# Last mixture of a four-part network: four places instead of two between TensorE and ScalarE, with TensorE three halves ahead

## The chip, the cores and the metric

The kernel runs on one core of one Trainium2 chip. The metric is the device time of one execution in microseconds, as the median of several runs. A core has five engines with instruction streams of their own that meet only through semaphores: TensorE (PE: matmuls and transposes, results to PSUM), VectorE (DVE), ScalarE (ACT), GpSimd (POOL, here mostly issuing indirect DMAs) and SyncE (SP, issuing plain DMAs). PSUM has eight banks of 128 partitions x 512 fp32.

## The reference

Two layers of cross attention and a feed-forward mixture over x of 2 x 1024 tokens of 256 values; what matters here is the last part, a mixture with three routers:

```python
x_flat = x.reshape(B * T, D)
x_addr = x_flat @ P_w.T
dw1 = _route_dense(x_addr @ U1.T, K, TAU)   # top 3 of 12, softmax over the 3
dw2 = _route_dense(x_addr @ U2.T, K, TAU)
dw3 = _route_dense(x_addr @ U3.T, K, TAU)
h = _apply_mixture(x_flat, dw1, W1)         # sum_e dw[n,e] * (W[e] @ x[n])
h = jax.nn.gelu(h, approximate=False)
y = _apply_mixture(h, dw2, W2)
y = y + dw3 @ b2
```

with W1 of 12 x 1024 x 256, W2 of 12 x 256 x 1024, all in fp32. Each of 2048 tokens goes to three experts of the 12, by one router for W1 and by another for W2.

## The kernel before, in words

The mixture (`top3_mixture`) sorts the 2048 x 3 pairs of token and expert by expert into LT = 59 tiles of 128 rows, so that a tile has one expert (`owner`). The hidden vector of 1024 values is worked on in two halves of HH = 512.

**First products** (`expand(n)`, L2046; n from 0 to 117, the first 59 with the first half of W1, then 59 with the second half, "the second part"). GpSimd gathers token rows, TensorE transposes them (L2034, first part only) and multiplies a tile with its expert's weights into a bank of `psH` (n % 2). ScalarE copies the bank (`products`, L2141) into one of four places `po` in `shared`, and SyncE stores it to DRAM (L2299). TensorE waits for the copy of the product before last (`po_ready`, n - 1). Meanwhile GpSimd gathers three rows per token from what is stored (L1692, `W<-p_d,f_rows`), VectorE adds them up with their weights (`combine`, L2246 to L2249), and SyncE stores the sums (L2311). There are 16 sums per half; those of the first half run beside the first products' second part, those of the second half beside the first 52 halves of the second products.

Between the two come 16 small matmuls for `dw3 @ b2` (`bias`, L2063) through the banks of `psT` and `psY`.

**Second products.** The 59 tiles are worked on as 118 half tiles ("halves") in an order that `turns_of_products` makes: first the first half of tiles 0 to 51 (turns "first", 52 halves), then the second halves of these ("second"), and among them, spread evenly, seven whole tiles (52 to 58, "whole", two halves each). For each half m:

- GpSimd fetches the hidden rows from DRAM (`hidden(n)`, L1692 `shared<-h_d` or `sel<-h_d`) into one of up to seven seats `hg` (five in the later part). A fetch waits until the seat's last half has been transposed (`hT_mm`, `u.free`).
- TensorE transposes it (`turn_hidden(m)`, L2072, four transposes into `psV[m % 2]`), after waiting for the fetch (`hg_ld`) and for the gelu of m - 2 (`hT_ready`).
- ScalarE applies the gelu out of PSUM into `hT[m % 2]` (`hidden_T`, L2146), after waiting for the contraction of m - 2 (`y_mm`).
- TensorE contracts it with W2 (`contract(m)`, L2089, four matmuls of 128x256, eight records in the trace) into `psY[n % 2]`, n the turn.
- For the turns "first", ScalarE copies the result into `y_part` (`first_part`, L2150). For "second", VectorE adds it (L2268), for "whole" it copies (L2265); then GpSimd scatters the tile's rows to DRAM (`scatter`, L1988).

The orders are written out by hand. On TensorE:

```python
turn_hidden(0)
for m in range(TILES):          # 118
    if m + 1 < TILES:
        turn_hidden(m + 1)
    contract(m)
```

ScalarE has the same order with `hidden_T(m + 1)` ahead of `first_part(m)`. GpSimd alternates one hidden fetch with one gather for the sums in the first parts (`three`), and from turn 58 on `hidden(n)` with `scatter(n - 6)`; after the last fetch the last six scatters follow. After all scatters the pairs come back from DRAM and are weighted and added (L2125, L2276, L2281), and the tiles are stored.

PSUM is full: `psT`, `psH`, `psV` and `psY` of two banks each. During the first products `psV` holds the routing's counts and lists, and SBUF has little room left.

Of the kernel before, what the change touches and what calls it, by code (L numbers as in the profile page):

```python
# [6 lines left out]
ALU = mybir.AluOpType  # L7
# [53 lines left out]
LATE = 4  # L61
TT = B * NT
# [66 lines left out]
def build(nc, t, out):  # L129
# [41 lines left out]
    with ctx:  # L171
# [9 lines left out]
        def attention_weights(stack, a):  # L181


            w = sb(stack, a + "W", [P, 4, KD, D])
            return [w] + [w[:, i] for i in range(4)] + [sb(stack, a + n, shape) for n, shape in (
                ("bk", [P, KD]), ("bq", [P, KD]), ("bvr", [1, D]))]
# [44 lines left out]
        def bias_row(eng, l, done):  # L231
            eng.dma_start(att[l][7][:, :], t[f"a{l}_bv"].rearrange("(a d) -> a d", a=1)).then_inc(done, 16)
# [115 lines left out]
        def value_products(pe, Wv, bvr, place):  # L348
            for b in range(B):
                for k in range(KD):  # L350
                    pe.matmul(place(b), ctxT[:, k, b * S2:(b + 1) * S2], Wv[:, k, :], start=k == 0, stop=False)
                mm = pe.matmul(place(b), ones[0:1, 0:S2], bvr[:, :], start=False, stop=True)
# [1163 lines left out]
        def top3_mixture(W, W1, W2, Pw, U, w_ld, w1_ld, w2_ld, load_w1_part, finite):  # L1516
# [9 lines left out]
            with st:  # L1526
# [21 lines left out]
                under = sb(st, "f_under", [P, E1 + 1, E1])  # L1548
                spread = sb(st, "f_spread", [P, E1 + 1, E1])
# [5 lines left out]
                first = sb(st, "f_first", [P, TT])  # L1555
# [10 lines left out]
                pdiv = sb(st, "f_pdiv", [P, TOP, TT])  # L1566
                pmod = sb(st, "f_pmod", [P, TOP, TT])
# [167 lines left out]
                with main:  # L1735
# [11 lines left out]
                    hT = xh.rearrange("p (s k n) -> p s k n", s=2, k=KQ)  # L1747
# [4 lines left out]
                    b2 = sb(main, "f_b2", [P, D])  # L1752
# [202 lines left out]
                    with nc.Block() as block:  # L1955
# [68 lines left out]
                        def _(pe):  # L2024
# [13 lines left out]
                            def expand(n):  # L2038
# [5 lines left out]
                                wait(pe, po_ready, n - 1)  # L2044
                                for k in range(KD):
                                    mm = pe.matmul(psH[:, n % 2, :], xTk[:, i, k, :], W1[c][:, e, k, :],  # L2046
# [19 lines left out]
                            def turn_hidden(m):  # L2066
# [3 lines left out]
                                wait(pe, hT_ready, m - 1)  # L2070
                                for k in range(KQ):
                                    mm = pe.transpose(psV[:, m % 2, k * P:(k + 1) * P],  # L2072
# [3 lines left out]
                            def contract(m):  # L2076
# [6 lines left out]
                                if n < 2:  # L2083
                                    pe.wait_ge(b_done, TT)
                                elif m == u.half:
                                    pe.wait_ge(ya_ready, min(n - 1, FIRST))
                                    wait(pe, yo_ready, n - 1 - FIRST)
                                for k in range(KQ):
                                    mm = pe.matmul(psY[:, n % 2, 0:D], hT[:, m % 2, k, :], W2[c][:, e, k, :],  # L2089
# [361 lines left out]
```

## Time and profile before

| | us |
|---|---|
| three timed runs, median (lowest, highest) | 1159.28 (1157.64, 1161.54) |
| span of the profiled execution | 1216.9 |
| first products' second part (734 to 840) | 106 |
| second products (849.0 to 1187.3) | 338.3 |
| of these: first parts, to 1009 | 160 |
| of these: second parts and whole tiles | 178 |
| return of the pairs, end (from 1188) | 29 |

The profile is one execution, recorded instruction by instruction. TensorE is its busiest engine (90% of the span). A record's span does not include the time at which its semaphore is seen elsewhere; that shows in when the next engine starts. Idle time of an engine is put down to what ended it.

### The profile page before, as it was taken

What the parts mean: (1) busy time and instruction counts of PE and PEld (TensorE: products, weight loads), DVE (VectorE), ACT (ScalarE), POOL (GpSimd) and SP (SyncE); (2) the same over time, 40 slices, a digit from 0 to 9 for tenths busy, and PEclk for the clock granted to TensorE, in tenths of its full rate; (3) what the DMA queues carried; (4) which work ended last, traced back from release to release, by engine and by line L of the source; (5) the groups of instructions that cost most, each with busy time, mean ns of one, the idle gap of its engine ahead of it and who ended that gap; (6) DMA issues with size and microseconds to landing.
All of it is one profiled execution on the core that took longest, in us unless ns stands there. A gap on an engine that the chain in (4) does not pass through costs nothing.

```text
span 1216.9 us, 19171 instructions
## 1 busy us (share of the span) xinstructions
PE 1094.3 (90%) x6013; PEld 817.2 (67%) x6013; DVE 552.3 (45%) x1120; ACT 420.3 (35%) x833; POOL 381.8 (31%) x421
## 2 busy tenths in 40 slices
PE   7999899998999999999399999998677888888885
PEld 4888744888998878887244443444566777776773
DVE  4988766764444446776872501333122211111114
ACT  1566544321112225664244432332222232222220
POOL 0221100000220011011154434552666646665650
PEclk8999999998999999999599999998898899999998
DMA  7000130004980029001155578997778865444437
GB/s 208 2 0 0 33 139 1 1 1 161 345 286 9 0 66 382 27 0 47 37 180 200 186 211 295 349 364 276 249 253 278 269 201 179 134 131 142 132 121 281
DMA packets 93410, 187.89 MB, mean 154 GB/s; under 512 B 14109, under 2 KB 34575, under 8 KB 93340
## 3 DMA queue, kind: packets, MB, share of 16 engines
q1 hardware_dynamic: 65346, 109.45, 25.4%
q0 software_dynamic: 23696, 73.69, 19.6%
q10 hardware_dynamic: 4298, 3.81, 1.0%
q8 instruction: 45, 0.74, 0.2%
q14 instruction: 25, 0.20, 0.0%
HBM read 133.56 MB, written 55.44 MB: 155 GB/s over the span
## 4 chain that ended last, share of the span: by engine, by line
PE 40%; issue 4%; DMA 4%; DVE 2%; another core or an unknown queue 2%; ACT 1%; SPq 0%; POOL 0%; POOLq 0%; DVEq 0%; ACTq 0%
PE f_psY L2089 18%; PE f_psH L2046 15%; PE f_psV L2072 4%; DMA W<-in_f_W1T 2%; DMA W<-p_d 2%; PE f_psT L2034 1%; ACT a_W L2146 1%; DVE W L1650 1%; PE f_psV L83 1%; DMA shared<-h_d,f_half_toks 0%; PE f_psH L1929 0%; PE f_psV L1662 0%; SPq L2343 0%; DVE f_xTk L2268 0%
## 5 line engine op out<-in xcount | busy, mean ns | idle before, releaser
L2089 PE MATMUL f_psY<-W,a_W 128*128 x944 | 240.7, 401 | 57.4 <-issue 35.6
L2089 PEld LDWEIGHTS f_psY<-W,a_W 128*128 128x128 f32 x944 | 179.4, 200 | 87.0 <-issue 65.4
L2046 PE MATMUL f_psH<-W,f_xTk 128*128 x472 | 215.5, 596 | 5.7 <-ACT shared L2141 2.0
L2046 PEld LDWEIGHTS f_psH<-W,f_xTk 128*128 128x128 f32 x472 | 84.1, 190 | 96.0 <-issue 95.6
L2146 ACT ACTIVATE a_W<-f_psV 128x512 f32<-128x512 f32 x118 | 70.0, 598 | 155.8 <-PE f_psV L2072 94.8
L2141 ACT ACTIVATE shared<-f_psH 128x512 f32<-128x512 f32 x118 | 70.4, 597 | 142.1 <-PE f_psH L2046 109.5
L1692 POOL DMA_INDIRECT W<-p_d,f_rows x96 | 95.0, 989 | 64.7 <-issue 24.7
L1692 POOL DMA_INDIRECT shared<-h_d,f_half_toks x90 | 87.6, 974 | 85.4 <-DMA p_d<-shared 25.6
L2246 DVE TENSOR_SCALAR a_W<-W,f_wt 128x512 f32<-128x512 f32 x32 | 15.9, 496 | 204.7 <-DMA W<-p_d,f_rows 147.6
L2268 DVE TENSOR_TENSOR f_xTk<-f_psY,f_xTk 128x256 f32<-128x256 f32 x52 | 21.7, 424 | 144.1 <-PE f_psY L2089 112.5
L1692 POOL DMA_INDIRECT a_W<-xn_d,f_toks x59 | 57.6, 975 | 88.9 <-PE f_psT L2034 54.3
L1510 POOL DMA_DIRECT2D m_eos<-m_eo x32 | 16.8, 527 | 202.0 <-DVE m_eo L1407 200.7
L700 POOL TENSOR_TENSOR X<-X,a_bob 128x256 f32 x32 | 24.4, 765 | 162.7 <-DVE a_xn L579 82.6
L1988 POOL DMA_INDIRECT p_d<-f_xTk,f_dest x59 | 58.4, 990 | 45.9 <-DVE f_xTk L2268 25.5
L2072 PE MATMUL f_psV<-ident,shared 128*128 128x128 f32 x360 | 56.5, 282 | 2.3 <-DMA shared<-h_d,f_half_toks 1.7
L1360 PE MATMUL m_psE<-m_eos,m_wu 128*128 128x256 f32 x256 | 57.8, 380 | 0.4 <-DVE m_wu L1436 0.4
L1131 PE MATMUL m_psL<-m_seT,shared 128*128 128x512 f32 x128 | 57.4, 592 | 0.0
L310 POOL TENSOR_TENSOR rstd<-veps,mhalf 128x8 f32<-128x8 f32 (+4 forms) x8 | 13.6, 1696 | 136.7 <-DVE veps L303 136.7
L2072 PEld LDWEIGHTS f_psV<-ident,shared 128*128 128x128 f32 x360 | 46.9, 147 | 13.1 <-DMA shared<-h_d,f_half_toks 2.6
L735 ACT ACTIVATE a_pT<-a_psP 128x256 f32<-128x256 f32 (+2 forms) x96 | 46.8, 490 | 20.2 <-PE a_psP L838 19.0
L2150 ACT ACTIVATE f_xTk<-f_psY 128x256 f32<-128x256 f32 x52 | 20.0, 384 | 93.5 <-PE f_psY L2089 54.0
L1360 PEld LDWEIGHTS m_psE<-m_eos,m_wu 128*128 128x128 f32 x256 | 47.5, 190 | 6.5 <-DVE m_wu L1436 0.7
(299 smaller groups left out, 1867.8 us busy)
## 6 DMA issues: line engine op xcount, KB each, us to landing
p_d<-shared SPq DMA_DIRECT2D x118, 256.0 KB
W<-in_f_W1T SPq DMA_DIRECT2D x24, 512.0 KB, 8.8
W<-in_f_W2T SPq DMA_DIRECT2D x24, 512.0 KB
m_wg<-in_m_Wg SPq DMA_DIRECT2D x16, 512.0 KB, 4.0
m_wu<-in_m_Wu SPq DMA_DIRECT2D x16, 512.0 KB, 5.2
m_wd<-in_m_Wd SPq DMA_DIRECT2D x16, 512.0 KB, 6.1
h_d<-a_W SPq DMA_DIRECT2D x32, 256.0 KB
W<-p_d SPq DMA_DIRECT2D x16, 384.0 KB, 9.2
```

What stands on the lines that cost most here:

```text
L700: pool.tensor_tensor(X[:, s, j], X[:, s, j], bob[:, :], ALU.add).then_inc(xb_ready, 1)
L735: act.activation(pT[:, s, full[0]:full[-1] + 1, :].rearrange("p c n -> p (c n)"), psP[:, g % 2 if g < 2 else 1, 0:len(full) * P], ACT.Copy ...
L1131: mm = pe.matmul(psL[:, n % 2, q * BANK:(q + 1) * BANK], xT[:, n % 2, k, :], seT[:, k, q * BANK:(q + 1) * BANK], start=k == 0, stop=k == K ...
L1360: mm = pe.matmul(psY[:, s, 0:D], ecT[:, s, c, :], eos[:, s, c, :], start=c == 0, stop=c == CS - 1)
L1692: pool.indirect_dma_start(place, None, source, bass.IndirectOffsetOnAxis(ap=index, axis=0)).then_inc(done, 16)
L1988: pool.indirect_dma_start(p2_rows, bass.IndirectOffsetOnAxis(ap=dest[:, i:i + 1], axis=0), y_part[:, i, :], None).then_inc(yo_stored_diag ...
L2046: mm = pe.matmul(psH[:, n % 2, :], xTk[:, i, k, :], W1[c][:, e, k, :], start=k == 0, stop=k == KD - 1)
L2072: mm = pe.transpose(psV[:, m % 2, k * P:(k + 1) * P], hg[u.seat + m - u.half][:, k * P:(k + 1) * P], ident[:, :])
L2089: mm = pe.matmul(psY[:, n % 2, 0:D], hT[:, m % 2, k, :], W2[c][:, e, k, :], start=k == 0 and not (whole and c == 1), stop=k == KQ - 1 and ...
L2141: act.activation(po[:, n % QUAD, :], psH[:, n % 2, :], ACT.Copy).then_inc(po_ready, 1)
L2146: act.activation(hT[:, m % 2].rearrange("p k n -> p (k n)"), psV[:, m % 2, :], ACT.Gelu).then_inc(hT_ready, 1)
L2268: dve.tensor_tensor(y_part[:, u.tile, :], psY[:, n % 2, 0:D], y_part[:, u.tile, :], ALU.add).then_inc(yo_ready, 1)
```

## The change

The constants WIDE = 4 and LEAD = 3 are new. In the second products the transposed halves go round four banks (`wide`: the two of `psV` and the two of `psH`), the gelus write four places `hT` (two new ones in `f_hT_more`), the results go round four banks (`y_banks`: `psY` and `psT`), and TensorE and ScalarE work three halves ahead instead of one. In the first products' second part the results go round the four banks of `wide` too; the third and fourth are free there once the lists are made (`list_ready`). To make room in SBUF, `under`, `spread`, `first` and `pmod` of the routing move into the weights' late space (`carve`), `pdiv` onto `pk`, and `b2` onto the second attention's `bvr`, which gets 128 partitions. GpSimd's and SyncE's orders stay.

```diff
+WIDE = 4
+LEAD = 3
...
-                under = sb(st, "f_under", [P, E1 + 1, E1])
-                spread = sb(st, "f_spread", [P, E1 + 1, E1])
+                under, spread = (carve((E1 + 1) * E1).rearrange("p (a e) -> p a e", e=E1) for _ in range(2))
...
-                first = sb(st, "f_first", [P, TT])
+                first = carve(TT)
...
-                pdiv = sb(st, "f_pdiv", [P, TOP, TT])
-                pmod = sb(st, "f_pmod", [P, TOP, TT])
+                pdiv = pk
+                pmod = carve(TOP * TT).rearrange("p (k t) -> p k t", k=TOP)
...
-                    hT = xh.rearrange("p (s k n) -> p s k n", s=2, k=KQ)
+                    hT_more = sb(main, "f_hT_more", [P, 2, HH])
+                    hT = [a.rearrange("p (k n) -> p k n", k=KQ) for a in (
+                        xh[:, 0:HH], xh[:, HH:2 * HH], hT_more[:, 0, :], hT_more[:, 1, :])]
...
-                    b2 = sb(main, "f_b2", [P, D])
+                    b2 = att[1][7]
...
+                    wide = [psV[:, 0, :], psV[:, 1, :], psH[:, 0, :], psH[:, 1, :]]
+                    y_banks = [psY[:, 0, 0:D], psY[:, 1, 0:D], psT[:, 0, 0:D], psT[:, 1, 0:D]]
+                    def product_bank(n):
+                        return psH[:, n % 2, :] if n < LT else wide[(n - LT) % WIDE]
+
+                    def hidden_bank(m):
+                        return wide[(LT + m) % WIDE]
...
-                                wait(pe, po_ready, n - 1)
+                                if n < LT:
+                                    wait(pe, po_ready, n - 1)
+                                elif n < LT + 2:
+                                    pe.wait_ge(list_ready, 1)
+                                elif n < LT + WIDE:
+                                    pe.wait_ge(po_ready, LT)
+                                else:
+                                    pe.wait_ge(po_ready, n - WIDE + 1)
...
-                                wait(pe, hT_ready, m - 1)
+                                if m < WIDE:
+                                    pe.wait_ge(po_ready, 2 * LT - WIDE + 1 + m)
+                                else:
+                                    pe.wait_ge(hT_ready, m - WIDE + 1)
...
-                                if n < 2:
+                                if n < WIDE:
                                     pe.wait_ge(b_done, TT)
                                 elif m == u.half:
-                                    pe.wait_ge(ya_ready, min(n - 1, FIRST))
-                                    wait(pe, yo_ready, n - 1 - FIRST)
+                                    pe.wait_ge(ya_ready, min(n - WIDE + 1, FIRST))
+                                    wait(pe, yo_ready, n - WIDE + 1 - FIRST)
...
-                            turn_hidden(0)
+                            for m in range(LEAD):
+                                turn_hidden(m)
                             for m in range(TILES):
-                                if m + 1 < TILES:
-                                    turn_hidden(m + 1)
+                                if m + LEAD < TILES:
+                                    turn_hidden(m + LEAD)
                                 contract(m)
...
-                                wait(act, y_mm, m - 1)
+                                wait(act, y_mm, m - WIDE + 1)
```

On TensorE, at the start of the second products: `ident,shared` are the transposes of a fetched half (a row x8 is two halves), `TENSOR_LOAD f_owner` begins a contraction. Before:

```order
L2063 MATMUL f1_psY<-f_b2,shared 128x256 x2
L2072 MATMUL f1_psV<-ident,shared 128x128 x8
L2080 TENSOR_LOAD f_owner
L2080 ISA x2
L2081 ISA
```

And changed:

```order
L2081 MATMUL f1_psY<-a1_bvr,shared 128x256 x2
L2093 MATMUL f1_psH<-ident,shared 128x128 x4
L2093 MATMUL f1_psV<-ident,shared 128x128 x8
L2093 MATMUL f1_psH<-ident,shared 128x128 x4
L2101 TENSOR_LOAD f_owner
L2101 ISA x2
L2102 ISA
```

Four halves are transposed ahead of the first contraction where it was two; from there on one half is transposed ahead of each contraction in both.

On ScalarE at the same place: `a1_W` and `f_hT_more` hold the gelus, `f_xTk` the copies of first parts. Before:

```order
L2146 ACT_TABLE_LOAD
L2146 ACTIVATE a1_W<-f1_psV 128x512 x2
L2150 ACTIVATE f_xTk<-f1_psY 128x256
L2146 ACTIVATE a1_W<-f1_psV 128x512
L2150 ACTIVATE f_xTk<-f1_psY 128x256
```

And changed:

```order
L2168 ACT_TABLE_LOAD
L2168 ACTIVATE a1_W<-f1_psH 128x512
L2168 ACTIVATE a1_W<-f1_psV 128x512
L2168 ACTIVATE f_hT_more<-f1_psV 128x512
L2168 ACTIVATE f_hT_more<-f1_psH 128x512
L2172 ACTIVATE f_xTk<-f1_psY 128x256
L2168 ACTIVATE a1_W<-f1_psH 128x512
L2172 ACTIVATE f_xTk<-f1_psY 128x256
```

The copy of the first result now stands behind four gelus instead of two.

## Rows read from the trace of the kernel before

**Rows 1.** The page's head and its busy time of TensorE.
```profile
span 1216.9 us, 19171 instructions
PE 1094.3 (90%) x6013; PEld 817.2 (67%) x6013; DVE 552.3 (45%) x1120; ACT 420.3 (35%) x833; POOL 381.8 (31%) x421
```

**Rows 2.** Busy time by stage; columns in the first line.
```profile
core 0: us, PE busy (x) PEld busy (x) DVE busy (x) ACT busy (x) POOL busy (x), PEclk, DMA share, GB/s
734.00:840.00 106.00, 102.89 (x242) 43.52 (x240) 32.13 (x48) 34.93 (x59) 48.29 (x48) 1.00 0.96 338
849.00:1009.00 160.00, 128.29 (x628) 108.41 (x628) 31.96 (x48) 47.97 (x105) 98.66 (x102) 0.90 0.77 250
1009.00:1188.00 179.00, 151.69 (x783) 128.64 (x781) 24.70 (x59) 44.76 (x89) 109.53 (x113) 0.97 0.42 136
```

**Rows 3.** Quiet stretch: chain of waits (start, us, what); then ScalarE's timeline.
```profile
995.15 0.44 PE f_psV L2072 x4
995.59 1.73 PE f_psY L2089 x8
...
997.75 1.73 PE f_psY L2089 x8
...
995.62 0.60 ACT L2146 ACTIVATE a_W<-f_psV 128x512 f32<-128x512 f32 x1
```

**Rows 4.** Timeline of a disturbed stretch: start, us, engine, line, operation, [idle before <-releaser].
```profile
1077.13 0.60 PE L2072 MATMUL f_psV<-ident,sel 128*128 128x128 f32 x4
1077.57 1.89 PE L2089 MATMUL f_psY<-W,a_W 128*128 x8
1082.78 0.60 ACT L2146 ACTIVATE a_W<-f_psV 128x512 f32<-128x512 f32 x1 [5.88 <-remote]
1083.55 0.42 DVE L2268 TENSOR_TENSOR f_xTk<-f_psY,f_xTk 128x256 f32<-128x256 f32 x1 [1.79 <-remote]
1083.58 2.98 PE L2089 MATMUL f_psY<-W,a_W 128*128 x8 [3.68 <-ACT a_W L2146]
```

**Rows 5.** GpSimd's issues by line: duration in ns min/median/max, first and last start.
```profile
L1692 POOL DMA_INDIRECT W<-p_d,f_rows x96: 942/949/1277, 738.7 to 982.4; - x96
L1692 POOL DMA_INDIRECT shared<-h_d,f_half_toks x90: 941/971/1270, 843.1 to 1168.9; - x90
L1692 POOL DMA_INDIRECT sel<-h_d,f_half_toks x14: 945/948/1270, 851.8 to 983.6; - x14
L1692 POOL DMA_INDIRECT sel<-h_d,f_toks x7: 967/971/971, 1016.4 to 1171.5; - x7
L1988 POOL DMA_INDIRECT p_d<-f_xTk,f_dest x59: 970/990/1008, 1012.5 to 1187.6; - x59
```

**Rows 6.** Waits of GpSimd, 985 to 1188: us in total, times, longest.
```profile
POOL p_d L1988 <- DVE f_xTk L2268: 25.5, 15, 2.7
POOL shared L1692 <- PE f_psV L2072: 18.6, 7, 10.4
POOL shared L1692 <- issue: 13.7, 45, 0.3
POOL p_d L1988 <- DVE f_xTk L2265: 6.8, 4, 2.9
POOL shared L1692 <- remote: 5.2, 3, 2.0
```

**Rows 7.** Waits in 734 to 841, of TensorE and ScalarE.
```profile
ACT shared L2141 <- DMA p_d<-shared: 11.2, 7, 2.9
PE f_psH L2046 <- ACT shared L2141: 1.8, 2, 0.9
PE f_psH L2046 <- issue: 1.1, 2, 0.9
```

**Rows 8.** Timeline: the first fetch of the second products and the first transposes.
```profile
843.07 0.94 POOL L1692 DMA_INDIRECT shared<-h_d,f_half_toks  x1 [25.62 <-DMA p_d<-shared]
846.85 0.72 PEld L2072 LDWEIGHTS f_psV<-ident,shared 128*128 128x128 f32 x4 [2.13 <-DMA shared<-h_d,f_half_toks]
```

More of the change, by code:

```diff
@@ L231, in bias_row @@
         def bias_row(eng, l, done):
-            eng.dma_start(att[l][7][:, :], t[f"a{l}_bv"].rearrange("(a d) -> a d", a=1)).then_inc(done, 16)
+            eng.dma_start(att[l][7][0:1, :], t[f"a{l}_bv"].rearrange("(a d) -> a d", a=1)).then_inc(done, 16)
         def half_batch(eng, b, h):
@@ L351, in value_products @@
                     pe.matmul(place(b), ctxT[:, k, b * S2:(b + 1) * S2], Wv[:, k, :], start=k == 0, stop=False)
-                mm = pe.matmul(place(b), ones[0:1, 0:S2], bvr[:, :], start=False, stop=True)
+                mm = pe.matmul(place(b), ones[0:1, 0:S2], bvr[0:1, :], start=False, stop=True)
             return mm
@@ L2043, in expand @@
                                 pe.wait_ge(xT_ready, i + 1)
-                                wait(pe, po_ready, n - 1)
+                                if n < LT:
[6 more added lines that the diff above has]
+                                    pe.wait_ge(po_ready, n - WIDE + 1)
                                 for k in range(KD):
-                                    mm = pe.matmul(psH[:, n % 2, :], xTk[:, i, k, :], W1[c][:, e, k, :],
+                                    mm = pe.matmul(product_bank(n), xTk[:, i, k, :], W1[c][:, e, k, :],
                                                    start=k == 0, stop=k == KD - 1)
@@ L2166, in _ @@
                                 products(LT + i)
-                            hidden_T(0)
+                            for m in range(LEAD):
+                                hidden_T(m)
                             for m in range(TILES):
-                                if m + 1 < TILES:
-                                    hidden_T(m + 1)
+                                if m + LEAD < TILES:
+                                    hidden_T(m + LEAD)
                                 if m < FIRST:
@@ L2264, in _ @@
                                     dve.wait_ge(y_mm, u.half + 2)
-                                    dve.tensor_copy(y_part[:, u.tile, :], psY[:, n % 2, 0:D]).then_inc(yo_ready, 1)
+                                    dve.tensor_copy(y_part[:, u.tile, :], y_banks[n % WIDE]).then_inc(yo_ready, 1)
                                 else:
                                     dve.wait_ge(y_mm, u.half + 1)
-                                    dve.tensor_tensor(y_part[:, u.tile, :], psY[:, n % 2, 0:D], y_part[:, u.tile, :], ALU.add
+                                    dve.tensor_tensor(y_part[:, u.tile, :], y_banks[n % WIDE], y_part[:, u.tile, :], ALU.add
                                                       ).then_inc(yo_ready, 1)
```

12 lines of the change are left out of this document (6 added, 6 removed).

## The prediction

> **What bounds the kernel now.** I read the page's totals first, then busy time by stage, then inside the last mixture's second products the repeating rhythm, the disturbed places, and the waits of the queue that feeds them.
>
> The profiled execution has a span of 1216.9 us, while the three timed runs have a median of 1159.28 [rows 1]. The profiled one is thus 57.6 us longer than what is timed. That difference decides this case, because the change aims at stalls of which the profile may hold more than a timed run does.
>
> By stage [rows 2]: the first products' second part (734 to 840) has TensorE busy for 102.9 of 106 us at full clock, with the DMA engines 96% busy. The second products run from 849.0 to 1187.3, in which TensorE is busy for 128.3 of 160 and 151.7 of 179 us, granted clock 0.90 and 0.97. What does TensorE need there? In a quiet stretch one half tile is four transposes (0.44) and eight matmul records (1.73), so 2.17 us, over and over [rows 3]. 118 halves are 118 x 2.167 = 255.7 us. The stage takes 338.3, so 82.6 us are gaps and slow clock.
>
> The quiet stretch also tells what the two places cost when nothing disturbs. ScalarE's gelu of the next half runs from 995.62 to 996.22, and the contraction that wants it starts at 997.75 [rows 3]: 1.53 us of slack. Two places are enough there. Elsewhere they are not [rows 4]. The transposes of 1077.13 end by the record at 1077.73, but their gelu starts at 1082.78, 5.05 us late; the contraction of 1077.57 to 1079.46 is picked up by VectorE only at 1083.55, 4.09 us late. TensorE itself stands still from 1079.9 until 1083.58. It waits for a gelu that waits for a signal that TensorE should long have given. Neither ScalarE nor VectorE is slow (0.60 and 0.43 us); the signal is late, and by more than 1.53 us.
>
> The other limit is GpSimd's queue. From 843.07 on it issues 90 + 14 + 7 fetches of hidden halves, 48 gathers for the sums (half of the 96) and 59 scatters [rows 5], each with 0.30 us behind it ("issue" in rows 6 is 13.7 us over 45). With 0.97, 0.95 and 0.99 us of their own these are 111 x 1.26 + 48 x 1.25 + 59 x 1.29 = 276 us, against 345.5 from the first start to the end of the last scatter at 1188.6. So GpSimd stood idle for some 69.5 us, most of it for TensorE's and VectorE's results [rows 6]. With no idle time of GpSimd and all else as profiled, the span would be 1216.9 - 69.5 = 1147.4. The timed median is only 11.9 us above that.
>
> **Are the late signals in the timed runs?** TensorE is busy for 1094.3 us of the span [rows 1], of which 280.0 are in this stage; outside it, it is busy for 814.3 of 877.9 us. 63.6 us idle remain for all other stages together, some of which are waits that no run can be without. So the 57.6 us can't well be missing there; most must be missing in the second products, where 82.6 us are lost. Taking them all from here leaves a stage of 280.7 us, near GpSimd's 276 and with 25 us above TensorE's 255.7. I conclude that the timed runs hold few of the late signals. This is an inference from two totals, not something that a row shows.
>
> The Trainium skill speaks against this: "NOTIFIC — the notification-queue block", Constraints, capacities, measured rates, says that a trace record of an instruction costs the engine no cycles. By it the stalls would be the kernel's own, and the sum would be the first rival's. No row here shows the record path. Another rule of the Trainium skill, in "Perfetto Trace Analysis", Optimization Strategy, reads a repeating gap on the engine that should be saturated as a sign of too few places in SBUF or PSUM; the quiet stretch with the same two places disagrees.
>
> **The change part by part.**
>
> No instruction is added. TensorE, ScalarE, VectorE and GpSimd run the same matmuls, gelus, copies and transfers; the moves of small tables into the weights' late space, of `pdiv` onto `pk` and of the bias matrix onto the attention's row keep their shapes: 0.
>
> First products' second part: results go round four banks instead of two. TensorE waited there for ScalarE for 1.8 us and once or twice more for 1.1 in total, while ScalarE waited 11.2 us for stores out of its ring of four [rows 7]. The ring is unchanged and the DMA engines are 96% busy [rows 2], so a TensorE that gets ahead is soon held by stores. Between 0 and -2.9 us; I take -1, nearer to the DMA-bound end. The new wait on the finished lists is met: the late weight loads before it had to wait for the same signal.
>
> Second products, late signals absorbed: TensorE stands three halves ahead, so the slack grows from 1.53 to 1.53 + 2 x 2.17 = 5.9 us, more than the 5.05 of [rows 4]. In the profiled execution this should be worth tens of microseconds, down to GpSimd's floor (-69.5 at most). In a timed run it can be worth at most the 11.9 us above that floor, at least 0. I take -2, near zero, because the quiet row is the nearest to a run without late signals.
>
> Second products, the price of the lead: the transposes of half m+3 stand ahead of the contraction of half m on TensorE, and the transposes wait for a fetch. A fetch takes 3.8 us from its start to the transposes that it releases [rows 8]. Queued behind that wait are now three contractions whose inputs are ready instead of one; behind them wait VectorE's sums, and behind those GpSimd's scatters, which sit between the fetches (a scatter of turn n-6 ahead of the fetch of turn n+1). At the start three more fetches of 1.25 us precede the first contraction, which costs nothing, as GpSimd doesn't wait for it. At the change from first parts to second parts the first scatter waits for a contraction that comes two transposes later (0.9 us) if TensorE has a backlog, or two whole halves later (4.3 us) if it has lived from fetch to fetch. At the end, with the last fetch landed, four contractions remain instead of two: 0 if TensorE has a backlog, 2 x 1.73 = 3.5 if not. Between +0.9 and +7.8; I take +2, nearer to the first, because in the profile TensorE is behind at both places: GpSimd waits 18.6 us for its transposes [rows 6].
>
> Sum: -1 - 2 + 2 = **-1 us**, 1158 us.
>
> **The rivals.**
>
> Faster: the late signals are partly the kernel's own. For it: they cost most of 82.6 us here, and nothing on the page marks them as foreign; timed runs may be shorter elsewhere by clock. Against it: the 57.6 us. Recovering 10 of the 11.9 us gives 1149; if other stages are shorter in timed runs than in the profile, the floor is lower too, to about 1140.
>
> Slower: TensorE has no backlog in timed runs. Per second-part turn GpSimd issues a fetch and a scatter, 1.26 + 1.29 = 2.55 us, against 2.17 of TensorE; in the first parts a fetch and a gather, 2.51. So without late signals TensorE lives from fetch to fetch, and the lead only holds finished work back: +4.3 at the change of parts and +3.5 at the end, 1167. It decides as soon as GpSimd and no longer TensorE is last at both places. Speaking against it: the seven whole tiles give GpSimd 4.33 us for one pair, and the sum then assumes that nothing is recovered.
>
> The change has no effect on the waits at all: it lands within the forecast's band.
>
> **How the numbers follow.** A measurement of this kernel can tell 0.3% (3.5 us) from no change. Forecast, within 0.3% of 1159.28: chance 0.44, its own range 1155.8 to 1162.8. Faster rival: 0.35, from 1140 to 1155.8. Slower rival: 0.21, from 1162.8 to 1167 and a little over. Leaving out a third of the faster cases' tail (below 1143) and some of the slower one's (above 1167) leaves out under 0.2. So 1143 to 1167.
>
> **What would show it.** In the profile after: the late signals still there (gelus 3 to 5 us behind their transposes), but TensorE's gaps ahead of the contractions (L2089 before) far smaller, the span down much more than the timed median, and GpSimd's waits for TensorE and VectorE shrunk from 56 us in the second parts. If span and timed median fall alike, the stalls were the kernel's own and my inference is wrong. If the slower rival holds, the chain ends with several contractions back to back after the last fetch, and the first scatter comes later behind the last fetch of the first seats. If the first products' second part is shorter by more than 3 us, its DMA bound was wrong.

## Result, and the profile after

| us, median (lowest to highest) | runs | time |
|---|---|---|
| before | 7 | 1159.65 (1157.64 to 1162.47) |
| after | 7 | 1166.36 (1163.11 to 1171.86) |

The ratio is 1.0059, with a 95% interval of 1.0039 to 1.0079. The kernel became 0.6% slower. The forecast was 1158.0, within 0.3% of no change; the time lies inside the stated range, on the side to which I had given 0.21.

The page's head and its line of busy times, after:

```profile
span 1165.6 us, 19169 instructions
PE 1081.1 (93%) x6013; PEld 807.6 (69%) x6013; DVE 552.6 (47%) x1120; ACT 424.5 (36%) x833; POOL 380.9 (33%) x421
```

The run of this profile took 1167.40. Span and timed median lie close together, which they did not in [rows 1]. So the kernel before was recorded again on the chip on which the first experiments ran:

> The kernel before, unchanged, for a second profile. If the 57 us between its first profile's span (1216.9) and its timed runs are an execution peculiar to the recording, the second profile's span is again some tens of us above the time of its unrecorded runs (1159.7), with gelus that start 2 to 5 us after their transposes' recorded end. If the stalls belong to the kernel and the first profile was only an unlucky execution, the span is about 1158, and the trace shows where a normal execution of it waits.

```profile
span 1161.4 us, 19171 instructions
PE 1081.8 (93%) x6013; PEld 806.9 (69%) x6013; DVE 552.9 (48%) x1120; ACT 424.1 (37%) x833; POOL 382.5 (33%) x421
```

That execution took 1163.25; the 19 timed runs on that chip have a median of 1160.97. The 57.6 us between [rows 1] and the timed median are simply not there. The Trainium skill ("NOTIFIC — the notification-queue block", Constraints, capacities, measured rates) says that a trace record costs the engine nothing, and both recorded runs agree with it: 2.3 and 1.0 us above their medians, within the scatter of single runs. What [rows 1 to 8] show is another kind of execution, and not the cost of recording, to which the fourth and fifth series come back. Where both kernels are compared on this kind of chip, "before" from here on is this second profile.

Busy time by stage, columns as in [rows 2]. Before, then after:

```profile
734.00:840.00 106.00, 103.22 (x241) 44.36 (x244) 32.09 (x48) 35.55 (x61) 48.35 (x48) 1.00 0.96 340
849.00:986.00 137.00, 123.12 (x630) 100.93 (x629) 32.07 (x48) 51.56 (x105) 100.54 (x103) 0.98 0.87 286
986.00:1133.00 147.00, 143.27 (x781) 124.17 (x780) 25.05 (x59) 45.13 (x88) 108.57 (x112) 1.00 0.52 170
```
```profile
734.00:840.00 106.00, 104.33 (x263) 47.41 (x261) 37.75 (x64) 36.47 (x60) 50.03 (x50) 0.99 0.95 340
846.00:984.00 138.00, 124.06 (x633) 103.50 (x632) 32.07 (x48) 51.66 (x106) 97.96 (x101) 0.97 0.86 286
984.00:1138.00 154.00, 144.60 (x771) 122.78 (x769) 25.05 (x59) 43.97 (x86) 108.54 (x111) 1.00 0.47 158
```

From the first contraction to the end of the last, the second products took 338.3 us in the first profile. Undisturbed they take 283 before (849.2 to 1132.0) and 290 after (846.2 to 1136.5): after, they start 3 us earlier and end 4.5 us later.

There are no late signals after, and there were none before to absorb: in neither profile does any wait have the releaser "remote", which the waits of [rows 4] have. The place of [rows 4] in the profile after (timeline: start, us, engine, line, operation, idle before it and what ended it):

```profile
1077.52 0.60 PE L2093 MATMUL f_psH<-ident,shared 128*128 128x128 f32 x4
...
1077.96 1.89 PE L2110 MATMUL f_psY<-W,a_W 128*128 x8
1078.16 0.60 ACT L2168 ACTIVATE a_W<-f_psH 128x512 f32<-128x512 f32 x1 [1.28 <-PE f_psH L2093]
...
1079.89 0.42 DVE L2291 TENSOR_TENSOR f_xTk<-f_psY,f_xTk 128x256 f32<-128x256 f32 x1 [1.74 <-PE f_psY L2110]
```

The transposes end at 1078.12 and their gelu starts 0.04 us later, where it was 5.05 in [rows 4]; the sum starts 0.04 us behind its contraction, where it was 4.09.

GpSimd's waits in the second parts answer [rows 6]. Before (985 to 1135), then after (965 to 1140):

```profile
POOL p_d L1988 <- DVE f_xTk L2268: 5.3, 11, 1.3
POOL p_d L1988 <- DVE f_xTk L2265: 2.9, 1, 2.9
```
```profile
POOL p_d L1999 <- DVE f_xTk L2291: 12.2, 8, 5.0
POOL p_d L1999 <- DVE f_xTk L2288: 7.6, 7, 2.5
```

The scatters of GpSimd's queue waited 8.2 us for VectorE, now 19.8. Of the seven whole tiles, before, only the last keeps its scatter waiting longer than the 0.30 us that lie between any two issues. After (L2288), five of the other six do so as well, with 0.53 to 1.21 us.

### The profile page after: what moved, and what is told of

It reads as the page before. It is cut to its first block, busy times and chain, and to the rows that moved or that the text cites. A ratio compares the mean times of both kernels' runs of the same rounds, so it can differ in the third digit from the quotient of the medians.

```text
span 1165.6 us, 19169 instructions
## 1 busy us (share of the span) xinstructions
PE 1081.1 (93%) x6013; PEld 807.6 (69%) x6013; DVE 552.6 (47%) x1120; ACT 424.5 (36%) x833; POOL 380.9 (33%) x421
## 3 DMA queue, kind: packets, MB, share of 16 engines
q0 software_dynamic: 23696, 73.69, 19.8%
## 4 chain that ended last, share of the span: by engine, by line
PE 31%; DMA 8%; POOL 6%; issue 3%; DVE 2%; SPq 0%; ACT 0%; DVEq 0%; POOLq 0%; ACTq 0%
PE f_psH L2064 12%; PE f_psT L2110 5%; PE f_psV L2064 4%; PE f_psY L2110 4%; DMA shared<-h_d,f_half_toks 3%; DMA sel<-h_d,f_toks 2%; POOL W L1693 2%; POOL shared L1693 2%; DMA W<-p_d 2%; PE f_psH L2093 1%; PE f_psV L2093 1%; DMA p_d<-shared 1%; PE f_psT L2045 1%; POOL p_d L1999 1%; POOL sel L1693 1%
## 5 line engine op out<-in xcount | busy, mean ns | idle before, releaser
L2064 PE MATMUL f_psH<-W,f_xTk 128*128 x352 | 163.6, 594 | 2.3 <-ACT f_xTk L2157 1.4
L2269 DVE TENSOR_SCALAR a_W<-W,f_wt 128x512 f32<-128x512 f32 x32 | 16.2, 507 | 186.6 <-DMA W<-p_d,f_rows 142.3
L2064 PEld LDWEIGHTS f_psH<-W,f_xTk 128*128 128x128 f32 x352 | 62.3, 190 | 59.8 <-issue 59.8
L2110 PE MATMUL f_psY<-W,a_W 128*128 x352 | 86.9, 391 | 3.9 <-issue 1.8
L2163 ACT ACTIVATE shared<-f_psH 128x512 f32<-128x512 f32 x88 | 52.5, 598 | 100.2 <-PE f_psH L2064 94.5
L2110 PE MATMUL f_psT<-W,f_hT_more 128*128 x336 | 81.3, 385 | 2.3 <-issue 2.1
L2110 PEld LDWEIGHTS f_psY<-W,a_W 128*128 128x128 f32 x352 | 65.3, 196 | 13.7 <-issue 6.3
L2110 PEld LDWEIGHTS f_psT<-W,f_hT_more 128*128 128x128 f32 x336 | 61.0, 191 | 11.1 <-issue 4.4
L312 POOL TENSOR_TENSOR rstd<-veps,mhalf 128x8 f32<-128x8 f32 (+4 forms) x8 | 13.6, 1695 | 136.4 <-DVE veps L305 136.4
L2064 PE MATMUL f_psV<-W,f_xTk 128*128 x120 | 53.9, 592 | 0.0
L840 PE MATMUL a_psP<-ident,a_pr 128*128 128x128 f32 x320 | 47.4, 278 | 2.7 <-ACT a_pr L729 1.9
L729 ACT ACTIVATE a_pr<-a_sc 128x1232 f32<-128x1232 f32 x32 | 39.4, 1230 | 12.3 <-DVEq L609 12.3
```

The lines of the kernel that those rows point to most:

```text
L729: act.activation(pr[:, s, :], sc[:, s].rearrange("p h k -> p (h k)"), ACT.Exp).then_inc(p_ready, 1)
L840: mm = pe.transpose(psP[0:CHR[c], g if g < 2 else 1, (c - cs[0]) * P:(c - cs[0] + 1) * P], pr[:, s, c * P:c * P + CHR[c]], ident[:, :])
L2064: mm = pe.matmul(product_bank(n), xTk[:, i, k, :], W1[c][:, e, k, :], start=k == 0, stop=k == KD - 1)
L2110: mm = pe.matmul(y_banks[n % WIDE], hT[m % WIDE][:, k, :], W2[c][:, e, k, :], start=k == 0 and not (whole and c == 1), stop=k == KQ - 1 an ...
L2163: act.activation(po[:, n % QUAD, :], product_bank(n), ACT.Copy).then_inc(po_ready, 1)
```

## Experiments

**First series (chip 15; before 1160.97): which part costs what.** `lead1` has all four places, but TensorE and ScalarE work one half ahead, as before the change:

```diff
-LEAD = 3
+LEAD = 1
```

> The change with LEAD = 1: four places everywhere, but transposes and gelus only one half ahead as before. Theory A (the order is what costs: contractions held behind transposes that wait for a fetch, scatters late, GpSimd idle): the loss of 6.7 us is gone, 1157 to 1160. Theory B (the places or their banks cost, or the first products' part does): as slow as the change, 1164 to 1168.

`first_only` changes the first products' second part alone; the second products keep two places and the lead of one:

```diff
-LEAD = 3
+LEAD = 1
...
-                        return wide[(LT + m) % WIDE]
+                        return psV[:, m % 2, :]
...
-                                    pe.wait_ge(hT_ready, m - WIDE + 1)
+                                    pe.wait_ge(hT_ready, m - 1)
...
-                                wait(act, y_mm, m - WIDE + 1)
+                                wait(act, y_mm, m - 1)
```

> Only the first products' second part goes round four banks; the second products as before with two places, one half ahead. Theory A: 1156 to 1160, since the profile of the change shows TensorE without a gap there (101.7 us for 59 halves) and the first fetch 2.7 us earlier. Theory B, if this part is the cause through DMA congestion: 1164 or more.

`second_only` changes the second products alone:

```diff
-                        return psH[:, n % 2, :] if n < LT else wide[(n - LT) % WIDE]
+                        return psH[:, n % 2, :]
...
-                                    pe.wait_ge(po_ready, n - WIDE + 1)
+                                wait(pe, po_ready, n - 1)
```

> Only the second products are changed (four places, three ahead); the first products as before. Theory A: as slow as the change or up to 2.7 us slower, 1165 to 1169. Theory B with the first products' part as the cause: 1158 to 1161.

| | us | ratio (95%) |
|---|---|---|
| lead1 | 1156.87 | 0.9964 (0.9949 to 0.9980) |
| first_only | 1155.96 | 0.9950 (0.9933 to 0.9967) |
| second_only | 1172.12 | 1.0086 (1.0069 to 1.0104) |

The two halves of the change pull in opposite directions: -5.0 and +11.2, together +6.2, where the whole change measures +6.7 (seven runs against seven). With a lead of one, four places do nothing that two don't: `lead1` and `first_only` are 0.9 us apart. So the loss comes from the lead, not from the places or from the moved tables. `second_only` is 3 us slower than even its slower expectation allowed, which had counted on 2.7 us for the first products and not on 5.0.

Where the lead costs its time is read from four marks in each profile, all on GpSimd: the starts of the first fetch of a hidden half, of the first scatter, of the last fetch and of the last scatter. They are read to a tenth, so a difference can be off by 0.1 us.

| us | first fetch at | to first scatter | to last fetch | to last scatter | all three |
|---|---|---|---|---|---|
| before | 843.3 | 144.6 | 132.3 | 12.6 | 289.5 |
| first_only | 836.6 | 142.3 | 132.4 | 12.5 | 287.2 |
| lead1 | 835.0 | 144.0 | 132.6 | 12.7 | 289.3 |
| second_only | 842.4 | 147.1 | 135.6 | 16.1 | 298.8 |
| after | 837.9 | 147.4 | 136.0 | 16.0 | 299.4 |

`second_only` against before: +2.5, +3.3 and +3.5 us, three places of nearly equal weight. They sum to 9.3, of which the earlier first fetch takes 0.9, which leaves 8.4 of the 8.7 us by which the spans differ (1170.1 and 1161.4). The timed medians differ by 11.2; the profiled execution of before was 2.3 us above its median.

The end, in the timeline after:

```profile
1121.35 0.97 POOL L1693 DMA_INDIRECT sel<-h_d,f_toks  x1 [0.31 <-issue]
1126.07 0.66 PE L2093 MATMUL f_psH<-ident,sel 128*128 128x128 f32 x4 [0.66 <-DMA sel<-h_d,f_toks]
1127.19 1.99 PE L2110 MATMUL f_psT<-W,a_W 128*128 x8 [0.46 <-issue]
...
1129.45 3.62 PE L2110 MATMUL f_psY<-W,f_hT_more 128*128 x16
1132.91 3.62 PE L2110 MATMUL f_psT<-W,a_W 128*128 x16
...
1137.26 0.97 POOL L1999 DMA_INDIRECT p_d<-f_xTk,f_dest  x1 [2.47 <-DVE f_xTk L2288]
```

And before:

```profile
1120.23 0.97 POOL L1692 DMA_INDIRECT sel<-h_d,f_toks  x1 [0.30 <-issue]
1125.08 0.66 PE L2072 MATMUL f_psV<-ident,sel 128*128 128x128 f32 x4 [0.47 <-DMA sel<-h_d,f_toks]
1126.15 1.99 PE L2089 MATMUL f_psY<-W,a_W 128*128 x8 [0.42 <-issue]
1128.41 3.62 PE L2089 MATMUL f_psY<-W,a_W 128*128 x16
...
1132.77 0.97 POOL L1988 DMA_INDIRECT p_d<-f_xTk,f_dest  x1 [2.91 <-DVE f_xTk L2265]
```

In both the transposes start as soon as the last fetch lands; TensorE has no backlog. Behind them stand 8 and 16 contraction records before, and 8, 16 and 16 after: one row of 16 (two contractions, 3.62 us) more.

The change from first to second parts: the last fetch ahead of the first scatter and the scatter, with the transposes and the contraction of the half that it stores. After:

```profile
975.70 0.60 PE L2093 MATMUL f_psH<-ident,shared 128*128 128x128 f32 x4
...
979.42 0.95 POOL L1693 DMA_INDIRECT shared<-h_d,f_half_toks  x1 [0.30 <-issue]
...
982.63 1.89 PE L2110 MATMUL f_psY<-W,a_W 128*128 x8
...
985.34 1.00 POOL L1999 DMA_INDIRECT p_d<-f_xTk,f_dest  x1 [4.98 <-DVE f_xTk L2291]
```

And before:

```profile
981.96 0.66 PE L2072 MATMUL f_psV<-ident,shared 128*128 128x128 f32 x4 [0.17 <-DMA shared<-h_d,f_half_toks]
...
985.18 1.89 PE L2089 MATMUL f_psY<-W,a_W 128*128 x8
...
987.89 1.00 POOL L1988 DMA_INDIRECT p_d<-f_xTk,f_dest  x1 [1.33 <-DVE f_xTk L2268]
```

GpSimd stands for 4.98 us ahead of its first scatter; before it was 1.33, so 3.65 more. The half that it waits for is contracted 6.93 us after its transposes, before 3.22, so 3.71 more. In between TensorE does not stand still: it works off three other contractions and three other sets of transposes, before one of each.

A whole tile in the middle, after:

```profile
1006.10 0.42 DVE L2288 COPY f_xTk<-f_psY 128x256 f32<-128x256 f32 x1 [3.91 <-PE f_psY L2110]
...
1006.80 0.99 POOL L1999 DMA_INDIRECT p_d<-f_xTk,f_dest  x1 [1.16 <-DVE f_xTk L2288]
```

And before:

```profile
1026.10 0.42 DVE L2265 COPY f_xTk<-f_psY 128x256 f32<-128x256 f32 x1 [3.91 <-PE f_psY L2089]
...
1029.04 0.99 POOL L1988 DMA_INDIRECT p_d<-f_xTk,f_dest  x1 [0.30 <-DVE f_xTk L2268]
```

Both scatters are the whole tile's own: counted from the start of the second parts, copy and scatter are the 9th after and the 17th before (the releaser named in the last row is the sum of the next turn, which had ended last by then). Before, the copy has been done for 2.52 us when GpSimd comes to its scatter, and the scatter waits only for the gap. After, GpSimd waits 1.16 us, and the fetch behind it in the queue is late by the difference. Over the seven, the last one apart, these waits are 7.6 - 2.5 = 5.1 us, of which six gaps of 0.30 would be there anyway: 3.3 us. One scatter of an ordinary turn adds 0.36. That makes 3.7 us, the loss of the middle column (136.0 against 132.3).

The distance between a result and its scatter, paired by count in the two traces, shows how it comes about. Where neither engine waits it grows by 0.40 us a turn, and it falls by 1.76 us at a whole tile, which takes TensorE two contractions for one scatter. The least that occurs is 0.28. Before, it stands between 3.2 and 6.1 us ahead of the whole tiles in the middle, and none waits. After, it stands at 1.20, 1.82, 2.07, 1.37, 1.41 and 1.15, and all wait but the third, the only one above 2.04.

**Second series (chip 4; before 1216.27): is it the scatter's place in GpSimd's queue?** If the lead costs time only because scatter n - 6 comes too early for it, scatter n - 8 should give it back.

```diff
-                                if n >= FIRST + DEEP - 1:
-                                    scatter(n - DEEP + 1)
+                                if n >= FIRST + 8:
+                                    scatter(n - 8)
```

`lead3_lag8` is the change with this edit, `lead3_lag10` the same with 10, `first_lag8` is `first_only` with this edit, `lead2` the change with LEAD = 2.

> The change with the scatters moved two turns back in GpSimd's queue: turn n's fetch is followed by the scatter of turn n - 8 instead of n - 6; eight scatters are left for after the last fetch. In the change GpSimd waits 12.2 + 7.6 us for VectorE ahead of scatters, with fetches queued behind. Theory A (the fetches behind a scatter that waits for a held contraction are the main price): these waits move behind the last fetch, the stretch from first hidden fetch to first scatter and that over the seven whole tiles shrink together by 4 to 6 us, while the 3.5 us at the end stay: 1160 to 1163. Rival C (the lead costs through the fetches' own landing: transposes that wait for a fetch hold the contractions, and it doesn't matter what GpSimd issues in between): no change, 1165 to 1168.

> The change with LEAD = 2. Theory A: at the end three contractions are left instead of two (1.7 us, half of the lead-3 price), and a whole tile's scatter has 2.2 us more room than at lead 3, so GpSimd's 1.1 us wait at each of the seven is gone: 1157 to 1161. If the price were the lead's depth in proportion (rival C), half of what lead 3 costs over lead 1: 1161 to 1163.

> Only the first products' part of the change (as in first_only, 1156), with the scatters two turns back as in lead3_lag8. At one half ahead GpSimd waits only 5.0 + 2.9 us for VectorE, most of it after the last fetch. Theory A: 1154 to 1157, no difference from first_only that can be told, so that what the later scatters bring at lead 3 is the lead's price and not a gain of its own. If it falls by 4 us or more, the later scatters are a gain by themselves.

> Scatters four turns back, three halves ahead; one look. Theory A: nothing waits for VectorE ahead of the last fetch any more; last fetch to last scatter 16 us or somewhat more, since ten scatters of 1.29 us stand behind it (12.9 us): within 2 us of lead3_lag8.

| | us | ratio (95%) |
|---|---|---|
| lead3_lag8 | 1200.65 | 0.9883 (0.9855 to 0.9911) |
| lead2 | 1204.60 | 0.9903 (0.9876 to 0.9930) |
| first_lag8 | 1220.20 | 1.0030 (1.0008 to 1.0051) |
| lead3_lag10 | 1196.70 | one run |

The expectations were written for a kernel of 1160 us, and none of their absolute times fits: on this chip the kernel before, unchanged, takes 1216.27 in its timed runs, as long as the span of [rows 1]. The late signals are thus in timed runs too, on this chip. Here the lead helps: `lead3_lag8` and `first_lag8` have the same first products and the same order on GpSimd, and they are 19.6 us apart. `lead3_lag10` is a single execution and no more than a hint. For the other kind of chip the series says nothing, so its question was put again.

**Third series (chip 8; before 1159.95).**

> The change again, beside the variants, since the kernel before has taken 1160 in some series and 1216 in another, and variants can be compared only inside one series. In a series where before takes 1160: 1165 to 1168. In a series where before takes 1216, in which TensorE's completions are seen 2 to 5 us late, the lead hides them: theory A expects 1197 to 1206 (lead 2 took 1204.6, lead 3 with later scatters 1200.7); if the loss by the lead is the same in both, 1222.

> Scatters two turns back at lead 3, again. Series of 1160: theory A (fetches queued behind scatters that wait for held contractions are the main price) 1160 to 1163; rival C (the fetches' own landing) 1165 to 1168, as the change. Series of 1216: 1199 to 1202 as before.

> LEAD = 2 again. Series of 1160: theory A 1157 to 1161, rival C 1161 to 1163. Series of 1216: 1203 to 1206 as before.

> Only the first products' part of the change, with scatters two turns back. Series of 1160: theory A 1154 to 1157, as without the later scatters (1156.0). Series of 1216: about 1220 as before.

| | us | ratio (95%) | first fetch at | to first scatter | to last fetch | to last scatter |
|---|---|---|---|---|---|---|
| after_again | 1166.47 | 1.0049 (1.0033 to 1.0066) | 839.8 | 147.4 | 137.7 | 16.1 |
| lead3_lag8_b | 1159.02 | 0.9989 (0.9976 to 1.0002) | 838.3 | 147.5 | 127.2 | 16.0 |
| lead2_b | 1160.77 | 1.0003 (0.9989 to 1.0017) | 838.5 | 145.3 | 132.3 | 14.4 |
| first_lag8_b | 1155.36 | 0.9959 (0.9945 to 0.9973) | 838.7 | 145.6 | 128.3 | 12.5 |

Later scatters take 7.5 us off the change (1166.47 to 1159.02), more than expected, and without the lead they bring nothing: `first_lag8_b` is at -4.6 us against its before, `first_only` at -5.0 against its own. So they remove a cost of the lead, and no other. In `lead3_lag8_b` the first scatter stands two turns later in the queue, so two of the fetches lie on its other side; its column "to first scatter" therefore holds 2.5 us of issues that belong to the next one. GpSimd's waits in `lead3_lag8_b`, 838 to 1190:

```profile
POOL p_d L1999 <- DVE f_xTk L2291: 8.2, 13, 2.2
...
POOL p_d L1999 <- DVE f_xTk L2288: 2.5, 1, 2.5
```

The 12.2 and 7.6 us of after have become 8.2 and 2.5, and of the whole tiles only the last still keeps its scatter waiting. What stays is the end: 16 us from the last fetch to the last scatter with the lead of three, 14.4 with two, 12.6 with one, to 0.1 in all nine profiles without late signals: about 1.7 us per step of lead, a contraction of 1.73 each. `lead3_lag8_b` and `first_lag8_b`, which differ in the lead and in the places alone, are 3.7 us apart, about the 3.5 of the end. `lead2_b` lies at the border between its two expectations, so its time does not decide between them. Its marks do: the middle column is back at 132.3, and 5.7 us of the change's time are gone with one step of lead.

**Fourth and fifth series (chips 2 and 1; before 1222.95 and 1223.18): a lead that ends in time.** In `taper` TensorE runs three ahead and falls back to one for the last eight halves, while ScalarE's order stays; `taper_lag8` has the later scatters as well.

```diff
+                            turned = LEAD
                             for m in range(TILES):
-                                if m + LEAD < TILES:
-                                    turn_hidden(m + LEAD)
+                                ahead = LEAD if m < TILES - 8 else 1
+                                while turned <= m + ahead and turned < TILES:
+                                    turn_hidden(turned)
+                                    turned += 1
                                 contract(m)
```

> The change, but for the last eight halves TensorE falls back from three halves ahead to one. Theory A, third term (after the last fetch four contractions remain instead of two): last fetch to last scatter falls from 16.0 back to 12.5 us and the rest stays: 3.5 us less than the change, so 1162 to 1164 in a series where before takes 1160. Rival D (the last scatter's own queue or the landing sets the end): no change.

> All three prices of the lead taken away: three halves ahead, scatters two turns back in GpSimd's queue, one half ahead for the last eight. Theory A: the first products' gain is left alone, 1154 to 1157 in a series where before takes 1160, level with the first products' part alone (1156); in a series where before takes 1216, 1195 to 1198. If something of the lead's cost is still unnamed, it stays above 1158.

> The first products' part alone again, beside the two: 1155 to 1157 where before takes 1160; 1212 to 1220 where it takes 1216.

> The taper at the end again, for a series of the other kind. Where before takes 1160: theory A 1162 to 1164 (3.5 us below the change of the same series), rival D as the change. Where before takes 1216 or more: about 1.3% below before.

> Taper and later scatters again. Where before takes 1160: theory A 1154 to 1157; above 1158 something of the lead's price is still unnamed. Where before takes 1216 or more: about 1.7% below before.

> The change beside them. Where before takes 1160: 1165 to 1168. Where before takes 1216 or more (not yet measured there): taper took 1207 against 1223 of before, so theory A expects 1.0 to 1.3% below before, at most 3.5 us above taper, and the sign of the change turns with the series.

| | chip | us | ratio (95%) |
|---|---|---|---|
| taper | 2 | 1207.14 | 0.9871 (0.9840 to 0.9902) |
| taper_lag8 | 2 | 1202.86 | 0.9834 (0.9804 to 0.9865) |
| first_only_b | 2 | 1215.73 | 0.9934 (0.9914 to 0.9955) |
| taper_c | 1 | 1206.93 | 0.9877 (0.9856 to 0.9898) |
| taper_lag8_c | 1 | 1203.85 | 0.9848 (0.9827 to 0.9869) |
| after_c, the change itself | 1 | 1210.89 | 0.9911 (0.9889 to 0.9933) |

Both series fell on chips of the kind with late signals. The change itself is 0.9% faster there, where on chip 8 and in the first comparison it is 0.5 to 0.6% slower. The sign turns with the chip. The taper is worth 4.0 us against the change (1210.89 to 1206.93), about the 3.5 of the missing row of contractions. From the last fetch to the last scatter it does not show (17.5 and 15.4 us, the change 15.5), since late signals fall into that stretch too: in `taper` TensorE comes to the first half of the last fetch 10.6 us after the fetch's start, in `after_c` 4.4. From the last transposes on it does show. In `taper`:

```profile
1172.04 0.60 PE L2093 MATMUL f_psV<-ident,sel 128*128 128x128 f32 x4
1172.48 3.62 PE L2110 MATMUL f_psT<-W,a_W 128*128 x16
```

One row of 16 follows, as in before, and the last scatter starts at 1176.83, 4.8 us after the transposes. It is 4.8 or 4.9 in all four profiles with the taper and 4.8 in the second profile of before, and 8.2 in `after` and `after_c`. So the end costs 3.4 us, and the taper takes it away on this kind of chip. A kernel with taper and later scatters was not run on a chip without late signals. From 1159.02 and 3.5 us less I would estimate about 1155.5, no better than `first_only`.

Why does the lead not bring tens of microseconds on these chips? The waits in the profile of `after_c`, 843 to 1190, and below it those of GpSimd alone from 838 on:

```profile
ACT f_xTk L2172 <- remote: 47.8, 11, 7.9
```
```profile
POOL p_d L1999 <- DVE f_xTk L2291: 32.0, 15, 5.0
...
POOL p_d L1999 <- DVE f_xTk L2288: 7.1, 3, 2.5
```

And the timeline of a disturbed place in it:

```profile
1081.11 1.89 PE L2110 MATMUL f_psT<-W,a_W 128*128 x8
...
1082.83 0.60 PE L2093 MATMUL f_psV<-ident,shared 128*128 128x128 f32 x4
...
1083.27 1.89 PE L2110 MATMUL f_psT<-W,f_hT_more 128*128 x8
...
1085.44 1.89 PE L2110 MATMUL f_psY<-W,f_hT_more 128*128 x8
1085.56 0.76 DVE L2291 TENSOR_TENSOR f_xTk<-f_psT,f_xTk 128x256 f32<-128x256 f32 x2 [4.27 <-PE f_psT L2110]
1085.62 0.60 ACT L2168 ACTIVATE a_W<-f_psV 128x512 f32<-128x512 f32 x1 [3.43 <-PE f_psV L2093]
```

The transposes end at 1083.43 and their gelu starts at 1085.62, 2.19 us late. TensorE goes on meanwhile, as meant: it waited 18.8 us for gelus on such a chip before, and in `after_c` no such wait is among its larger ones. But VectorE is late as well: the contraction of 1081.11 ends at 1083.00, and its sum, the first of the two at 1085.56, starts 2.56 us later. GpSimd's scatters wait 39.1 us for VectorE, against 32.3 in the first profile of before. Its fetches wait for TensorE or have the releaser "remote" for 30.3 us, there 43.6. All of GpSimd's waits for the other engines thus come to 69.4 us against 75.9. The lead spares TensorE its standstills, but most of the wait in the queue that feeds TensorE stays. From first fetch to last scatter it was 344.5 us on such a chip and is 340.2.

## Why the prediction failed, by its own steps

**Late signals in the timed runs** (the inference from two totals): right. The second profile of before has 289.5 us from the first fetch to the start of the last scatter, [rows 5] has 344.5; that is 55.0 of the 55.5 us between the spans. The stage of 280.7 that I derived stands against 283. (I compared a span with a timed median. A timed value is some 1.8 us above the span of the same execution here, 1167.40 and 1165.6, so the 57.6 should be some 59 and the 11.9 some 10, which changes none of the steps.) "Late signals absorbed", taken at -2, was 0 where there are none; on the other kind of chip the second products gained about 5 us (`after_c` -12.3 against `first_only_b` -7.2, on two chips of equal time before). Wrong was what I expected to see: a profile after with late signals in it and a span far above the median.

**GpSimd's floor**: right as a count (276 us of issues), and it was nearer than I treated it. Before has 290.5 us to the end of its last scatter, only 14.5 above the floor. GpSimd was the bound of the second products, and TensorE its follower.

**First products' second part**, 0 to -2.9, taken at -1: mis-sized; `first_only` measures -5.0. The reason given was a DMA bound at 96%. The windows 736 to 828 of before and after show that it was none:

```profile
736.00:828.00 92.00, 89.32 (x206) 38.51 (x206) 31.62 (x48) 30.64 (x52) 48.35 (x48) 1.00 0.98 350
```
```profile
736.00:828.00 92.00, 92.00 (x215) 40.68 (x215) 32.25 (x48) 31.73 (x54) 48.24 (x48) 1.00 0.99 351
```

At the same transfer rate TensorE runs without a gap, which gives 2.7 us in this window, close to the upper end of my term. The whole second part takes it 101.4 us instead of 105.4. Its last product ends at 833.0 instead of 839.9; of these 6.9 us, 4.0 come from the second part, 1.3 were there at the very first product (611.4 and 610.1), and 1.6 arose in the first part, for which I had no term and no run gives a cause. Between 727 and 845 ScalarE still waits for stores (15.5 us, before 22.8), but TensorE waits for ScalarE no more (before 2.6 us). The chain of before holds one late store in full:

```profile
809.93 9.46 DMA p_d<-shared
...
819.48 0.61 ACT shared L2141
...
820.37 3.70 PE f_psH L2046 x8
```

Part of the gain is given back by the last store (3.54 us instead of 2.10) on the way to the first fetch.

**The price of the lead**, +0.9 to +7.8, taken at +2: this is the step that failed. `second_only` measures +11.2, beyond its upper end. It failed in two ways: in the choice within the range, and by a place that it left out. I took a value near the lower end "because in the profile TensorE is behind at both places" [rows 6]. That row came from an execution with late signals, which I had just argued away from the timed runs. Having concluded that they hold none, I had to price the lead for a TensorE without backlog, and that is the upper end: 4.3 and 3.5. The end measured 3.5, as worked out; the change of parts measured 2.5 (`second_only` against before) or 5.1 (`after` against `first_only`), on either side of the 4.3, and 3.7 by GpSimd's wait and by the delay of the contraction. The place left out is the middle: the scatters of the whole tiles, 3.3 to 3.7 us, had no term, so that even the upper end was too low.

**The slower rival** had the mechanism right (TensorE lives from fetch to fetch, the lead holds finished work back), and its 1167 is the measured time. The agreement is partly luck: it lacks 5 us of gain in the first products and 3.3 to 3.7 of loss in the middle. What I held against it, that the whole tiles give GpSimd 4.33 us for one pair, was the wrong reading: it is at the whole tiles that TensorE falls behind by two contractions for one scatter, and with the lead the scatter is due before it has caught up. The distances counted out above show this, and later scatters remove these waits (`lead3_lag8_b`).

**Faster rival**: it was right for the other kind of chip. There the change takes 12.3 us off, and the rival gave 10. Of the Trainium skill's rule for repeating gaps ("Perfetto Trace Analysis", Optimization Strategy) the runs say: more places alone changed nothing in the second products (`lead1`), and were worth 5 us in the first ones, where they were used without any lead (`first_only`).

Of the versions, `first_only` (0.9950), `first_lag8_b` (0.9959) and `lead1` (0.9964) beat both kernels where signals are prompt, and `taper_lag8` (0.9834 and 0.9848) is the fastest of those run several times where they are late. `first_only` is faster than before on both kinds. Later scatters without the lead are not to be had for nothing where signals are late: `first_lag8` was 0.3% slower than before on chip 4, which no theory of mine had expected and which stays open.

## What to carry to other kernels

In this kernel more places between two engines cost nothing; working further ahead did, by the work that is held back behind each transfer not yet landed: count it at the first and the last use and wherever another engine's queue alternates between feeding and draining. When span and timed median disagree, record the kernel again before pricing anything, and take no row of the disturbed execution as evidence for the undisturbed one. A DMA share of 96 to 99% did not say here that an engine beside it had nothing to gain.

## What the runs showed of the hardware

The same kernel takes 1160.0 to 1161.0 us on chips 8 and 15 and 1216.3 to 1223.2 on chips 4, 2 and 1, 5% apart, with single runs within 0.7% of their chip's median. The granted clocks of the whole runs are not far apart (0.96 and 0.97). The difference lies in one stage, the second products, where on the second kind of chip VectorE and ScalarE see TensorE's completion 2 to 5 us late, for stretches at a time. In this stage the clock differs too: 0.90 and 0.97 in [rows 2], 0.98 and 1.00 in the second profile. But TensorE is busy for 280.0 us in the first profile's stage and for 266.4 in the second's, so slower matmuls make up at most 13.6 of the 55 us. And in [rows 4] signals are late while the transposes (0.60 us) and the contraction (1.89) take as long as in the profile after. Whether the lower clock is more than a consequence of the standstills is not shown. In the profiles of that kind these waits appear with the releaser "remote":

```profile
ACT a_W L2146 <- remote: 43.1, 18, 5.9
```

This is the line of the first profile of before (843 to 1190); the second has no wait with that releaser. It is likely that the first profile was taken on a chip of the second kind, since its span is theirs, but its chip isn't recorded. Why signals are late there, and why in this stage only, stays open.
